# Waiting for the last but one landing ahead of each indirect DMA in an attention and mixture-of-experts block

## The reference

```python
x = x + attn(layernorm(x), Wq, bq, Wk, bk, Wv, bv, Wo, bo, m)   # linear attention, 16 heads of 8
x = x + ffn(layernorm(x), ...)

# ffn: top-1 of 16 experts, scaled by a sigmoid of the chosen logit, and a shared expert of width 512
logits = hidden @ router_w.T
top_vals, top_idx = jax.lax.top_k(logits, 1)
...
routed_in = hidden[None] * scores.T[:, :, None]
gate, up = split(einsum('nth,nhf->ntf', routed_in, gate_up_proj))
routed_out = einsum('ntf,nfh->nth', up * silu(gate), down_proj)
shared = silu(hidden @ shared_gate_w.T) * (hidden @ shared_up_w.T) @ shared_down_w.T
return shared + routed_out.sum(axis=0)
```

## Time and profile before

| | before |
|---|---|
| median of 3 runs | 298.6 us |
| the profiled execution, its time | 296.75 us |
| the profiled execution, its span | 294.6 us |
| PE busy | 214.8 us (73%) |
| DVE busy | 163.6 us (56%) |
| POOL busy | 140.6 us (48%) |
| ACT busy | 122.9 us (42%) |
| indirect DMAs (POOL) | 80, some 0.96 us each |
| granted TensorE clock, mean | 0.856 |

### The profile page before, as it was taken

The page is one execution under the profiler, slowest core; times in us unless marked ns, Lnnn a source line. Parts: engine busy times, 40 slices in busy tenths (PEclk is TensorE's granted clock), DMA queues, the critical chain, the costliest instruction groups (busy, mean ns, idle before and its releaser), DMA issues.

```text
span 294.6 us, 3483 instructions
## 1 busy us (share of the span) xinstructions
PE 214.8 (73%) x1067; PEld 171.9 (58%) x1067; DVE 163.6 (56%) x401; ACT 122.9 (42%) x238; POOL 140.6 (48%) x148
## 2 busy tenths in 40 slices
PE   1768988897778757984425699897568594689983
PEld 0437666585676745752413577696568493576761
DVE  2278899999818699732110366672425251045565
ACT  3325457675755875421010355451314231044460
POOL 8005748558571334777774000027466657564410
PEclk9995999999978777796577599999795869759998
DMA  4996110600000000111111100243223111102934
GB/s 133 300 392 213 37 37 1 196 21 0 1 2 0 0 0 0 48 55 45 54 54 57 51 2 0 72 103 105 63 92 103 49 38 55 45 36 70 291 105 142
DMA packets 27905, 22.58 MB, mean 77 GB/s; under 512 B 2400, under 2 KB 24944, under 8 KB 27888
## 3 DMA queue, kind: packets, MB, share of 16 engines
q1 hardware_dynamic: 22640, 15.85, 18.5%
q0 software_dynamic: 2560, 5.26, 5.0%
q10 hardware_dynamic: 2688, 1.25, 1.5%
HBM read 11.83 MB, written 10.53 MB: 76 GB/s over the span
## 4 chain that ended last, share of the span: by engine, by line
PE 35%; DVE 23%; another core or an unknown queue 15%; issue 15%; ACT 7%; POOL 4%; DVEq 0%; POOLq 0%; ACTq 0%
PE quad_banks L972 5%; PE quad_banks L970 5%; PE quad_banks L971 4%; PE bank L1118 4%; PE bank L1008 3%; DVE qkv L676 2%; DVE st L641 2%; DVE s_act L720 2%; PE quad_banks L926 2%; DVE ss L685 2%; PE bank L1009 2%; PE bank L1010 2%; DVE s_spl L725 2%; PE bank L916 1%
## 5 line engine op out<-in xcount | busy, mean ns | idle before, releaser
L435 POOL DMA_INDIRECT y_rows<-yg,home x48 | 45.9, 957 | 64.5 <-ACT yg L617 46.6
L720 DVE TENSOR_TENSOR s_act<-quad_banks,sg_act 128x512 f32<-128x512 f32 x32 | 22.0, 690 | 51.2 <-ACT sg_act L528 25.7
L528 ACT ACTIVATE sg_act<-quad_banks 128x512 f32<-128x512 f32 x32 | 19.0, 597 | 63.9 <-remote 32.3
L428 POOL DMA_INDIRECT x_slots<-h_rows,pos x32 | 32.1, 1002 | 13.6 <-issue 9.5
L376 POOL TENSOR_TENSOR qkv<-qkv,rn 128x512 f32<-128x512 f32 x16 | 16.9, 1075 | 33.6 <-DVE rn L693 33.6
L1008 PE MATMUL bank<-s_spl,sdT 128*128 128x512 f32 x32 | 16.6, 520 | 19.5 <-DVE s_spl L725 13.9
L1118 PE MATMUL bank<-w_dn,e_actT 128*128 x96 | 17.2, 337 | 18.3 <-DVE e_actT L887 18.3
L1118 PEld LDWEIGHTS bank<-w_dn,e_actT 128*128 128x128 f32 x96 | 15.3, 241 | 19.8 <-issue 19.8
L926 PE MATMUL quad_banks<-w_c,xT 128*128 128x384 f32 x64 | 25.0, 539 | 0.9 <-ACT w_c L537 0.6
L725 DVE TENSOR_TENSOR s_spl<-s_act,s_spl 128x512 fp32r<-128x512 f32 x32 | 22.0, 687 | 2.6 <-ACT s_spl L534 2.3
L1008 PEld LDWEIGHTS bank<-s_spl,sdT 128*128 128x128 f32 x32 | 7.0, 220 | 26.4 <-DVE s_spl L725 19.2
(11 more groups left out here) (156 smaller groups left out, 580.1 us busy)
## 6 DMA issues: line engine op xcount, KB each, us to landing
x_slots<-w_raw SPq DMA_DIRECT2D x8, 387.0 KB, 6.2
xg<-x_slots SPq DMA_DIRECT2D x12, 258.0 KB
xres<-L_attn_x SPq DMA_DIRECT2D x8, 256.0 KB, 5.4
w_raw<-L_ffn_gate_up_proj SPq DMA_DIRECT2D x4, 512.0 KB, 3.7
h_rows<-y_rows SPq DMA_DIRECT2D x8, 256.0 KB, 5.8
out<-xres SPq DMA_DIRECT2D x4, 256.0 KB, 3.9
out<-xres ACTq DMA_DIRECT2D x4, 256.0 KB, 2.6
y_rows<-yg,home POOLq DMA_INDIRECT x48
```

What stands on the lines that cost most here:

```text
L428: g.indirect_dma_start(out=x_slots, out_offset=bass.IndirectOffsetOnAxis(ap=pos[:, t:t + 1], axis=0), in_=h_rows[:, t, :], in_offset=None) ...
L435: g.indirect_dma_start(out=y_rows, out_offset=bass.IndirectOffsetOnAxis(ap=home[:, n:n + 1], axis=0), in_=yg[:, n, :], in_offset=None).the ...
L528: a.activation(sg_act[:, k % 2], pair[:, 2 * (k % 2)], ACT.Silu).then_inc(s_silu, 1)
L720: v.tensor_tensor(s_act[:, k % 2], pair[:, 2 * (k % 2) + 1], sg_act[:, k % 2], ALU.mult).then_inc(s_act_rdy, 1)
```

## The change

Each of the semaphores `scat` and `back` becomes a pair. DMA number t of a loop counts on number t % 2 of its pair, and from the third DMA on POOL first waits until that semaphore has the count of DMA t - 2. So DMA t starts only when DMA t - 2 has landed. SP waits for both of a pair, each for half the count. Nothing else changes: the same DMAs move the same rows in the same order.

```diff
-        hs_pool, scat = sem("hs_pool"), sem("scat")
+        hs_pool, scat = sem("hs_pool"), [sem("scat0"), sem("scat1")]
...
-        away_rdy, home_rdy, back = sem("away_rdy"), sem("home_rdy"), sem("back")
+        away_rdy, home_rdy, back = sem("away_rdy"), sem("home_rdy"), [sem("back0"), sem("back1")]
...
-            sp.wait_ge(scat, 16 * NT)
+            for landed in scat:
+                sp.wait_ge(landed, 16 * NT // 2)
...
-            sp.wait_ge(back, 16 * SLOT_TILES)
+            for landed in back:
+                sp.wait_ge(landed, 16 * SLOT_TILES // 2)
...
+                if t >= 2:
+                    pool.wait_ge(scat[t % 2], 16 * (t // 2))
                 g.indirect_dma_start(out=x_slots, out_offset=bass.IndirectOffsetOnAxis(ap=pos[:, t:t + 1], axis=0),
-                                     in_=h_rows[:, t, :], in_offset=None).then_inc(scat, 16)
+                                     in_=h_rows[:, t, :], in_offset=None).then_inc(scat[t % 2], 16)
...
                 for n in range(Q * g_no, Q * g_no + Q):
+                    if n >= 2:
+                        pool.wait_ge(back[n % 2], 16 * (n // 2))
                     g.indirect_dma_start(out=y_rows, out_offset=bass.IndirectOffsetOnAxis(ap=home[:, n:n + 1], axis=0),
-                                         in_=yg[:, n, :], in_offset=None).then_inc(back, 16)
+                                         in_=yg[:, n, :], in_offset=None).then_inc(back[n % 2], 16)
```

## The result

| | median, us | runs |
|---|---|---|
| before | 298.41 | 297.84 to 299.35, 4 |
| after | 286.68 | 283.33 to 291.56, 4 |

The ratio is 0.954 (95% interval 0.947 to 0.960): faster by 4.6%, where 304 us had been forecast. The time lies in the range given (285 to 311 us) and on the side of the rival "slower pace, no pile-up", which said 285. A median is over all runs of a kernel, a ratio compares only its undisturbed (fast) runs, so the two can differ a little. The profiled execution took 291.56 us, the longest of these four, against 296.75: the two traces explain 5.2 of the 11.7 us.

What follows compares the result with a forecast made beforehand. PE's results reaching ACT and DVE late during indirect DMA bursts were taken as the bound. Longer bursts were to cost 3.7 us (token scatter) plus 2.4 us (row scatter), 6.1 on 298.6: 304.7, rounded to 304 us, range 285 to 311.

Steps and rivals of the forecast that it cites:

- slower pace, no pile-up: Rival: longer gaps between indirect DMAs keep PE's lag from building in both scatters; a third regained gives 285 us; chance 0.32.
- What bounds the kernel: Whole kernel: PE's results reach ACT and DVE late during long indirect DMA bursts, up to 15.7 us in the token scatter.
- At most two are in flight: Both scatters: landing takes 1.70 to 2.29 us, under the 2.53 us of two starts, so the cap cuts off no queue.
- The price of a wait: Both scatters: waking POOL after a landing adds 0.45 us a pair, range nothing to 0.51; token scatter 6.8 us longer.
- Hidden directly: Longer scatters have cover: experts fill only behind 184 us, and over 10 us lies behind the row scatter; direct cost nothing.
- Each microsecond of a burst runs PE at the burst's rate: Both scatters: longer bursts lose PE work at fixed rates, 0.55 and 0.36 of each added microsecond; 6.1 us in sum.
- +3.7 us of the token scatter: Token scatter: cost through PE of a burst 6.8 us longer, at 1.45 against 3.25 matmuls in a microsecond.
- the rate falls by a sixth only: Objection to the faster rival, both scatters: the DMA rate falls by only a sixth, too little to clear PE's lag.
- No change: Rival: waking is hidden, or each indirect DMA costs PE's results a fixed amount; 298.6 us within 1.5; chance 0.25.
- Slower in full: Rival: PE's followers wait for each landing, so row bursts hand on all 6.8 us; 309 us in total; chance 0.10.

Runs made afterwards that it cites:

- x4: Kernel before with at most four DMAs in flight in the token scatter alone, wait in its own instruction; 262.17 us against 260.19, ratio 0.995.
- x2_ride: Kernel before with the cap of two in the token scatter alone, landing wait written first so it rides on the DMA; 262.69 us against 260.19, ratio 1.016.
- x_only: Kernel before with the change's cap of two in the token scatter alone; 271.12 us against 260.19, ratio 1.047.
- before_again: The kernel before, unchanged, profiled on chip 12; 259.38 us, beside 259.73 for the kernel before there.
- both_again: The whole change, unaltered, on chip 12; 281.68 us against 259.73 for the kernel before, ratio 1.090.
- x_only_2: Kernel before with the cap of two in the token scatter alone, on a chip with late PE results; 290.98 us against 300.22, ratio 0.970.
- gap10_both: Kernel before with ten one-column memsets on POOL ahead of each indirect DMA in both scatters, no landing wait; 282.27 us against 299.66, ratio 0.953.
- gap6_both: Kernel before with six one-column memsets on POOL ahead of each indirect DMA in both scatters, no landing wait; 286.57 us against 299.66, ratio 0.966.
- y_half: Kernel before with half of each expert row scattered and loaded back (256 bytes in place of 512), token scatter untouched; 300.79 us against 300.22.
- cap2_both_held: The change, with the landing wait in its own instruction ahead of each row scatter DMA too; 288.83 us against 297.34 for the kernel before.
- cap2_both_ride: The change, with the token scatter's landing wait written first, row scatter as in the change; 287.84 us against 297.34 for the kernel before, ratio 0.975.
- cap4_both_held: Kernel before with at most four DMAs in flight in both scatters, waits in their own instructions; 296.36 us against 297.34, ratio 1.006.

## Why the prediction was wrong

**What bounds the kernel.** Right for the chip that it was read on: PE's results come late while indirect DMAs run. It could not be seen there that the same kernel has no late results on other chips.

**At most two are in flight.** Nearly right: a cap of four cuts off nothing (x4), a cap of two only where a landing takes over 2.53 us (three long waits in the token scatter of x2_ride). The prediction took one landing for all.

**The price of a wait.** Mis-sized. 0.45 us for a pair, at most 0.51, was said; the pair quoted above takes 0.59 us more than before, and with the stalls the mean pace gives 2 x (1.64 - 1.31) = 0.66. For a steady pair the upper bound was nearly it: 2.3 us to the landing and 0.75 to wake are 3.05, and 1.79 + 1.26 = 3.05 us is the pair that comes again and again in x_only. Left out were the landings that come late. The token scatter grew by 10.4 us, not 6.8; its last start came at 170.55, not 164.6. In the row scatter three waits of four ride on their DMA, and yet the change lengthens it from 60.4 to 71.4 us on chip 12 (first to last start in before_again and both_again). On the result's chip it grew only from 71.6 to 73.0: there POOL had stood for 3.42, 2.83, 1.49, 2.50 and 3.54 us at the starts of bursts, and I read it so that most of the landing waits fell into time that was lost before.

**Hidden directly.** Failed for the token scatter. The cover (experts only behind 184 us) was made of the late results themselves. When they vanished, the shared blocks were through by about 160 us and PE stood 19.2 us for the tokens. On prompt chips there was no cover for either scatter: 11 us each.

**The step that failed.** "Each microsecond of a burst runs PE at the burst's rate": 1.45 matmuls in a microsecond was taken as a constant of bursts. It is a result of their pace: 1.45 at 1.31 us (48 / 33), 4.0 at 1.64 us (132 / 33). So the +3.7 us of the token scatter was in truth a gain; x_only_2, which has this half alone, measured it at 9.2 us (290.98 against 300.22), the longer scatter already paid.

**The rivals.** "Slower pace, no pile-up" held in the token scatter, and gap10_both, with gap6_both at half strength, shows it as a cause. Its objection, that the rate falls by a sixth only, failed twice: it fell by a fifth (1.31 / 1.64), and an eighth (1.31 / 1.51, gap6_both) already brings 105 matmuls. That its 285 us lie so near 286.68 is luck: it took a third of 41 us in both scatters, while nearly all of the token scatter's loss came back, most of it was lost again at the new bound, and nothing to be seen came back in the row scatter. "No change", and the rule of the Trainium skill, "SBUF — State Buffer", who interferes with whom, that a DMA never contends with a compute engine: on chip 12 the traces agree with it (3.6 matmuls in a microsecond with the bursts on), on the late chips they disagree, whatever the path may be; y_half shows that in the row scatter the bytes are not it. "Slower in full" did not happen; the row scatter lasted 1.4 us longer.

**What stays open.** What in a late chip delays PE's results, and why it depends on the distance of POOL's indirect DMAs. In the token scatter memsets in the gap cure it, so it is not POOL being busy, and halving the bytes of the row scatter changed nothing. That late results come free in step with POOL's starts (gap10_both) ties them to what POOL does for an indirect DMA, but nothing in the traces shows the path. Why an even 1.53 us cures the token scatter and not the row scatter is open too. Whether the row half of the change gains anything on a late chip was not measured by itself. That the two levels belong to the chips rests on five chips, one of them in two series. Beyond the error, no version was found that beats the change on late chips (gap10_both's interval contains the change's ratio), and none of those that gain there was seen to be free on prompt ones: cap2_both_held, cap2_both_ride, gap6_both and gap10_both were not run there.

## What to carry to other kernels

A rate read inside a disturbed stretch is not a constant of the work: before multiplying a longer burst by it, ask what sets it, and let the rival that moves the rate have its full price. Cover that consists of waits vanishes with the waits, so look at what would be late next without them. A wait on a landing costs little when it rides on the DMA and some 0.3 us a DMA when it stands in an instruction ahead of it; put the wait that is met last where it rides if the pace is the bound, and time a change of this kind on more than one chip.

## What the runs showed of the hardware

- One kernel takes 257 to 264 us on two chips and 291 to 307 us on two others (298 on the result's). No trace of either kind has a remote wait ahead of 107 us, before the first indirect DMA; the late chips have them behind it, the prompt ones none at all.
- On late chips ACT stood up to 24.1 us for a PE result (cap4_both_held) at a start each 1.27 us, and in the token scatter for none at one each 1.53 us (gap10_both) or 1.63 (x_only_2).
- In gap10_both all 27 late results came free 0.63 to 0.69 or 1.38 to 1.48 us after a start of an indirect DMA on POOL.
- An indirect DMA of 128 rows landed 2.2 to 2.3 us after its start in the median and up to 4.2 us at worst (x_only, both_again).
- An indirect DMA on POOL leaves 0.30 us to the next; three one-column memsets (0.18 us) fit in and move the start by 0.04 us, ten (0.42 us) by 0.27.
- A change can be 4.6% faster on one chip and 9.0% slower on another of the same kind, with the same instructions.
